# A two-block transformer kernel: the second router by eight-largest and match-replace, and the key stack's load behind the maxima rows

## The reference, cut to what matters

```python
# block 0, attention: 16 heads of depth 8, softmax over 256 keys
scores = einsum('bhtd,bhsd->bhts', q, k) / sqrt(8)
attn = softmax(scores); out = einsum('bhts,bhsd->bhtd', attn, v)
# block 0, feed-forward: 64 experts of hidden size 88, 4 of 8 groups, top 8 experts, plus a shared one
# block 1, attention: a recurrent delta rule over the 16 sequences as time steps
# block 1, feed-forward: 8 experts of hidden size 512 and a ninth gate that scales x itself
probs = softmax(x @ router_w + router_b)               # 9 values per token
top_v, top_i = top_k(probs, 2)                          # the two largest, first index wins a tie
gates = sum(one_hot(top_i, 9) * top_v[..., None], -2)   # 9 gates per token, 7 of them zero
out = einsum(gates[..., :8], y) + gates[..., 8:] * x
```

## Time and profile before

| what | value |
|---|---|
| median of 3 runs | 2077.13 us (2068.6 to 2082.84) |
| the profiled execution's own time | 2077.66 us |
| its span, first to last instruction | 2075.9 us |
| mean granted TensorE clock | 0.926 |
| PE, DVE, ACT, POOL busy | 88%, 70%, 39%, 33% of the span |
| attention | about 50 to 425 us |
| experts, first part | about 545 to 1595 us |

### The profile page before, as it was taken

How to read it: one execution, slowest core, us unless ns; L and a number is a source line. 1 busy time by engine, 2 the same in 40 slices (tenths; PEclk the granted TensorE clock), 3 DMA queues, 4 the chain that set the end, 5 groups by cost and what they waited for, 6 DMA issues and landing times. The chain is left out here.

```text
span 2075.9 us, 25471 instructions
## 1 busy us (share of the span) xinstructions
PE 1825.3 (88%) x7668; PEld 1083.9 (52%) x7668; DVE 1454.5 (70%) x2624; ACT 812.9 (39%) x1501; POOL 682.3 (33%) x610
## 2 busy tenths in 40 slices
PE   2888888851899999989899899998997998999999
PEld 1455455541566656556556465565564554555555
DVE  5776666548666686986968969869689577554444
ACT  1466565631433324324233243332432543443333
POOL 2011111100000491943737718447376076000000
PEclk9988887855799999999999999999998998999999
DMA  7544343010223353323333233333331000000000
GB/s 262 153 115 108 102 116 94 26 70 0 77 106 115 99 175 99 97 78 96 86 87 96 76 96 87 87 96 85 87 97 31 1 5 6 6 6 5 5 5 5
DMA packets 101223, 157.84 MB, mean 76 GB/s; under 512 B 11221, under 2 KB 49454, under 8 KB 97929
## 3 DMA queue, kind: packets, MB, share of 16 engines
q1 hardware_dynamic: 97495, 154.65, 25.3%
q10 hardware_dynamic: 1586, 1.30, 0.2%
q0 software_dynamic: 2048, 0.79, 0.2%
HBM read 123.27 MB, written 33.42 MB: 75 GB/s over the span
## 5 line engine op out<-in xcount | busy, mean ns | idle before, releaser
L1293 PE MATMUL psum<-e_hhi,e_ring 128*128 128x512 f32 x704 | 480.6, 683 | 40.9 <-DVE e_hm L1736 32.0
L1548 ACT ACTIVATE e_gu<-psum 128x512 f32<-128x512 f32 (+1 forms) x368 | 219.0, 597 | 668.1 <-PE psum L1295 527.4
L1302 PE MATMUL psum<-e_hm,w_d 128*128 128x512 f32 (+1 forms) x736 | 383.9, 604 | 14.8 <-DVE e_x L1665 12.2
L1732 DVE TENSOR_TENSOR e_gu<-psum,e_gu 128x512 f32<-128x512 f32 x352 | 241.3, 686 | 185.4 <-PE psum L1332 170.3
L1800 POOL TENSOR_TENSOR e_prod<-e_state,e_phi 128x512 f32<-128x512 f32 x256 | 356.2, 1430 | 5.5 <-DVE e_y L1605 3.2
L1768 DVE TENSOR_TENSOR e_hm<-psum,e_gu 128x512 f32<-128x512 f32 x256 | 175.3, 689 | 206.0 <-ACT e_gu L1573 154.3
L1294 PE MATMUL psum<-e_hhi,e_ring 128*128 128x512 f32 x704 | 282.6, 401 | 0.0
L1295 PE MATMUL psum<-e_hlo,e_ring 128*128 128x512 f32 x704 | 281.7, 400 | 0.0
L1412 PE MATMUL psum<-e_hm,w_gu 128*128 128x512 f32 x512 | 266.8, 607 | 8.6 <-DVE e_hm L1768 3.5
L1573 ACT ACTIVATE e_gu<-psum 128x512 f32<-128x512 f32 x256 | 152.4, 597 | 287.1 <-PE psum L1295 260.8
L1736 DVE TENSOR_TENSOR e_hm<-psum,e_gu 128x512 f32<-128x512 f32 x352 | 243.6, 692 | 12.1
(11 more groups left out here) (238 smaller groups left out, 2482.9 us busy)
## 6 DMA issues: line engine op xcount, KB each, us to landing
e_ring<-w_split SPq DMA_DIRECT2D x308, 256.0 KB, 2.6
qk_parts<-at_part SPq DMA_DIRECT2D x96, 192.0 KB, 2.7
w_split<-e_ring SPq DMA_DIRECT2D x44, 256.0 KB, 2.0
at_qs<-qk_parts SPq DMA_DIRECT2D x16, 576.0 KB
at_ks<-qk_parts SPq DMA_DIRECT2D x16, 576.0 KB
w_gu<-in_w SPq DMA_DIRECT2D x2, 2048.0 KB, 10.6
sel_buf_r<-w_split SPq DMA_DIRECT2D x14, 256.0 KB, 2.6
w_gu<-in_wg SPq DMA_DIRECT2D x1, 2904.0 KB
```

What stands on the lines that cost most here:

```text
L1293: pe.matmul(out, w_hi, x_hi, start=first, stop=False)
L1302: mm = pe.matmul(ps[:, ACC, :], weights_at(T, WD + P * j, P)[0:rows(j), :], hm[0:rows(j), slot(j), :], start=(j == 0), stop=(j == HT - 1))
L1548: a(act_g[0:r, j % 2, :], ps[0:r, GB[j % 2], :], ACT.Silu).then_inc(silu_done, 1)
L1732: ins = v.tensor_tensor(product, ps[0:r, UB[j % 2], :], act_g[0:r, j % 2, :], ALU.mult)
```

## The change

1. In attention, SP's `load_stacks` becomes two loads. The query stack is loaded as before. Then SP waits until half 1 of batch n-1's maxima rows has landed in `at_qs` (`nrows_in[1]`), and only then loads the key stack. The writes of the next batch's parts stand behind that wait in SP's list.
2. The ranking in block 1's router is replaced. At tile 36 four `max` instructions (one for each token tile, nine values in, the eight largest out) stand in place of three comparisons and mask products over 324 values. At tile 37 a `memset` makes the places 2 to 7 of the eight unmatchable and four `match_replace` mark the two largest, in place of an addition and a reduction over 324 values. `router_cut` tests for the mark. The input `less9` and its load are gone; a semaphore `router_turn` is raised twice on the way.

```diff
-            def load_stacks(buf):
-                for stack, q in ((qs, 0), (ks, 1)):
-                    sp.dma_start(stack[0:ROWS, buf, :, :], bounce[buf, q].rearrange("b a d h t -> (b a d) h t")).then_inc(stacked, 16)
+            def load_stack(buf, stack, q):
+                sp.dma_start(stack[0:ROWS, buf, :, :], bounce[buf, q].rearrange("b a d h t -> (b a d) h t")).then_inc(stacked, 16)
...
+                rows_in = held(f"rows_in_{k}", 16 * n)
...
                     sp.wait_ge(part_out, out)
-                    load_stacks((k + 1) % BUFS)
+                    load_stack((k + 1) % BUFS, qs, 0)
+                    if f["p2"]:
+                        sp.wait_ge(nrows_in[1], rows_in)
+                    load_stack((k + 1) % BUFS, ks, 1)
...
-EARLY_LOADS = ("wqkv", "wo", "wr", "b_r1", "less9", "sel1")
+EARLY_LOADS = ("wqkv", "wo", "wr", "b_r1", "sel1")
...
-                s.done(v.tensor_tensor(pairs(above), pa, pb, ALU.is_gt), False)
-                s.done(v.tensor_tensor(pairs(equal), pa, pb, ALU.is_equal))
-                per = lambda ap: ap.rearrange("p (t g) -> p t g", t=CT)
-                s.done(v.tensor_tensor(per(equal), per(equal),
-                                       T["less9"][:].rearrange("p g e -> p (g e)").unsqueeze(1).broadcast_to([P, CT, E1 * E1]), ALU.mult))
+                v.sem_inc(router_turn, 1)
+                for t in range(CT):
+                    s.done(v.max(top[:, t, :], pr[:, t, :]), t == CT - 1)

             def router_rank(s):
-                s.done(v.tensor_tensor(above, above, equal, ALU.add))
-                s.done(v.tensor_reduce(rank[:].rearrange("p t e -> p (t e)"), above.rearrange("p (g e) -> p g e", e=E1), AX.X, ALU.add))
+                s.done(v.memset(top[:, :, TOP1:8], UNMATCHED))
+                v.sem_inc(router_turn, 1)
+                for t in range(CT):
+                    s.done(v.match_replace(out=w1[:, t, :], in_to_replace=top[:, t, :], in_values=pr[:, t, :],
+                                           imm_value=TAKEN), t == CT - 1)

             def router_cut(s):
-                s.done(v.scalar_tensor_tensor(w0[:], rank[:], float(TOP1), pr[:], ALU.is_lt, ALU.mult))
+                s.done(v.scalar_tensor_tensor(w0[:], w1[:], TAKEN / 2, pr[:], ALU.is_lt, ALU.mult))
```

More of the change, by code:

```diff
@@ L1041 @@
 TOP1 = 2
-EARLY_LOADS = ("wqkv", "wo", "wr", "b_r1", "less9", "sel1")
+EARLY_LOADS = ("wqkv", "wo", "wr", "b_r1", "sel1")
 FFN0_LOADS = len(EARLY_LOADS) + 5
-ROUTER_STEPS = 16
+ROUTER_STEPS = 20
 WG, WU, WD = 0, HIDDEN_ALL, 2 * HIDDEN_ALL
@@ L1138, in experts @@
         pr, w0, w1 = (sb(f"e_{n}", [P, CT, E1]) for n in ("pr", "w0", "w1"))
-        rank = w1
-        above = nt[:].rearrange("p t d -> p (t d)")[:, 0:CT * E1 * E1]
-        equal = xc[:, 0:CT * E1 * E1]
+        top = sb("e_top", [P, CT, 8])
         parts = sb("e_parts", [P, CT, PARTS, E1], BF16)
@@ L1179, in experts @@
         r_step = sem("r_step")
+        router_turn = sem("router_turn")
         shifted = sem("shifted")
@@ L1625, in router_gates @@
                 s.done(v.tensor_tensor(pr[:], pr[:], over(rs[:]), ALU.mult))
-                pa = pr[:].unsqueeze(2).broadcast_to([P, CT, E1, E1])
-                pb = pr[:].unsqueeze(3).broadcast_to([P, CT, E1, E1])
-                pairs = lambda ap: ap.rearrange("p (t g e) -> p t g e", g=E1, e=E1)
-                s.done(v.tensor_tensor(pairs(above), pa, pb, ALU.is_gt), False)
-                s.done(v.tensor_tensor(pairs(equal), pa, pb, ALU.is_equal))
-                per = lambda ap: ap.rearrange("p (t g) -> p t g", t=CT)
-                s.done(v.tensor_tensor(per(equal), per(equal),
-                                       T["less9"][:].rearrange("p g e -> p (g e)").unsqueeze(1).broadcast_to([P, CT, E1 * E1]), ALU.mult))
-            def router_rank(s):
-                s.done(v.tensor_tensor(above, above, equal, ALU.add))
-                s.done(v.tensor_reduce(rank[:].rearrange("p t e -> p (t e)"), above.rearrange("p (g e) -> p g e", e=E1), AX.X, ALU.add))
+                v.sem_inc(router_turn, 1)
+                for t in range(CT):
+                    s.done(v.max(top[:, t, :], pr[:, t, :]), t == CT - 1)
+            def router_rank(s):
+                s.done(v.memset(top[:, :, TOP1:8], UNMATCHED))
[3 more added lines that the diff above has]
+                                           imm_value=TAKEN), t == CT - 1)
             def router_cut(s):
-                s.done(v.scalar_tensor_tensor(w0[:], rank[:], float(TOP1), pr[:], ALU.is_lt, ALU.mult))
+                s.done(v.scalar_tensor_tensor(w0[:], w1[:], TAKEN / 2, pr[:], ALU.is_lt, ALU.mult))
                 s.done(v.tensor_copy(parts[:, :, 0, :], w0[:]))
@@ L1844 @@
 NAMES = ("x_fm", "x_tm", "c_fm", "wmod", "w_qk", "b_qk", "w_v", "b_v", "w_fc", "b_fc", "b_o", "ident", "rot", "ident_bf",
-         "gate_w", "gate_b", "wg", "wu", "wd", "sd", "wqkv", "wo", "sel", "wr", "b_r1", "less9", "sel1", "w1", "w2")
+         "gate_w", "gate_b", "wg", "wu", "wd", "sd", "wqkv", "wo", "sel", "wr", "b_r1", "sel1", "w1", "w2")
 def adaln_two_blocks(nc, *args):
@@ L1861, in adaln_two_blocks @@
                                 bfc_col=[P, 1], bo_col=[P, 1], shift=[P, 4, BATCH], scale1=[P, 4, BATCH], gate=[P, 4, BATCH],
-                                eps=[P, 1], ga_bfc=[P, BATCH], ga_bo=[P, BATCH], wqkv=[P, QKV1], wo=[P, D], wr=[P, E1], b_r1=[P, E1],
-                                less9=[P, E1, E1]).items():
+                                eps=[P, 1], ga_bfc=[P, BATCH], ga_bo=[P, BATCH], wqkv=[P, QKV1], wo=[P, D], wr=[P, E1], b_r1=[P, E1]).items():
             sb(name, shape)
@@ L1928, in layout @@
     a["b_r1"] = f(np.broadcast_to(i["L1_ffn_router_b"], (P, E1)))
-    a["less9"] = f(np.broadcast_to(np.tril(np.ones((E1, E1), np.float32), -1), (P, E1, E1)))
     a["sel1"] = f(np.tile(np.broadcast_to(np.eye(E1)[:, :, None], (E1, E1, P)), (PARTS, 1, 1)).astype(bf16))
```

## The result

| | before | after |
|---|---|---|
| median | 2078.98 us, 4 runs (2068.6 to 2082.84) | 2000.52 us, 4 runs (1997.03 to 2004.95) |
| profiled execution's own time, span | 2077.66, 2075.9 | 2004.95, 2003.1 |
| granted clock, whole span | 0.926 | 0.948 |

The kernel is faster by 3.7%: the ratio is 0.9631, with a 95% interval of 0.959 to 0.9672. The forecast was 2013 us in a range of 1986 to 2048.

What follows compares the result with a forecast made beforehand. TensorE, 88% busy, was taken as the bound, standing still for late maxima rows in attention and VectorE's router comparisons in the experts; 34 + 31 = 65 us off 2077.66 gave 2013 us, range 1986 to 2048.

Steps and rivals of the forecast that it cites:

- Attention, 34 us forecast: Attention with the key stack loaded behind the rows: 17 us of waits plus 17 us of clock, 11 to 45.
- The rows are held by the key stack: Attention: half 1's rows' write is 3.1 us late behind the stack loads; afterwards it lands in 1.70 us.
- VectorE's L355 is next, a gain of 1.4 us a batch and not 2.5: Attention: TensorE then waits for VectorE's L355, so 1.4 us a batch is gained, 17 us for twelve batches.
- Half of the clock's 34 us comes back, 17: Attention: the lower clock level costs 34 us in all; half is taken as regained, 17 us, ends 0 and 34.
- rival A: Attention: the rows are not late because of the key stack, so attention gives nothing: 2047 us, chance 0.09.
- The router, 31 us forecast: Block 1's router with the new ranking: 26 us from six chunks plus 5 us from chunk 6, 22 to 51.
- MAX8 and match-replace cost what block 0's rows say, GpSimd or not: Router: four MAX8 take 0.37 us, match-replace 0.85 us, not held by GpSimd; 6 x 4.25 = 26 us gained.
- No gain by the clock: Router: VectorE sets the pace where the clock is 0.50, so nothing is taken for clock; upper end 16 us.
- Chunk 6, 5 us: Router in chunk 6: the wait is 2.89 us; a gain of 5 us with the clock, 2 to 9.
- B: Router: MAX8 and match-replace are held by GpSimd, so only attention pays: 2044 us, chance 0.09.
- D: Whole change: neither part pays, VectorE's and ScalarE's lists being just as late behind each repaired wait: 2075 us, chance 0.06.
- C: Attention: the wait moves from half 1's rows to half 0's and the kernel is slower: 2093 us, chance 0.04.

Runs made afterwards that it cites:

- experiment 1: The kernel before with only the attention part of the change, the key stack loaded after half 1's rows: 2037.0 us, ratio 0.981 to the kernel before.
- experiment 3: The changed kernel with the key stack's heads 0 to 7 loaded right behind the query stack, heads 8 to 15 behind the rows: 1995.24 us.
- Experiment 2: The kernel before with only the router part of the change: 2042.66 us, ratio 0.9844 to the kernel before.
- experiment 4: The changed kernel with both stacks loaded only after half 1's rows have landed: 2020.33 us, ratio 0.9723 to the kernel before.
- experiment 8: The changed kernel with attention's third rest behind the maxima of heads 8 to 11 and router_cut at tile 38 instead of 40: 1980.21 us.

## Why the prediction held, step by step

**Attention, 34 us forecast.** 36.6 in the profile, 36.3 between the means of three profiles with the old code and three with the new, 40 in experiment 1. *The rows are held by the key stack*: shown by experiments 1 and 3; landing after 1.73 us of idle time where 1.70 was forecast. *VectorE's L355 is next, a gain of 1.4 us a batch and not 2.5*: L263 waits 1.19 us, and TensorE's idle time fell by 1.3 a batch. Two of the 15 waits of the earlier trace rows were at head 0 and not at head 8 as the prediction read them, 2.6 of its 34.8 us. *Half of the clock's 34 us comes back, 17*: 1.6 us a batch is 19 for twelve. Both terms were right within 2 us; the second by luck, since no row carried the choice of "half". What was off is small: half 0's L460 comes 0.9 to 1.2 us later after its write and not 0.2, since the key load runs beside SP's writes. It cost next to nothing: TensorE's waits for the rows at head 0 sum to 1.3 us in the changed kernel and to 3.6 in experiment 1, against 2.6 before. That the rows "speak against" turns between queues, as the prediction says under rival A, doesn't follow: experiment 3 shows in which order the write was served, and not that such turns are absent.

**The router, 31 us forecast.** 34.2 in the profile. *MAX8 and match-replace cost what block 0's rows say, GpSimd or not*: 0.38 against 0.37 us, and the rank 0.89 (842.41 to the next product at 843.30) against 0.85. The rule of the Trainium skill that the prediction named ("SBUF — State Buffer", Who interferes with whom) agrees, with 152 ns beside GpSimd. Counted from L1628 (L1625 before), tile 37's product comes 3.95 us earlier, tile 38's 4.07 and tile 41's still 4.08, so VectorE does set the pace here, as the forecast had it: 4.1 of 5.6 us. *TensorE would wait about 0.7 us*: 0.89. *No gain by the clock*: here the step failed in its reason and, by 1.5 us a chunk, in its size. TensorE's wait for the second product fell by 4.2 us, but 2.3 of it moved to L1393 (0.78 before, 3.16 after in chunk 0), where time at the lower clock, 6.8 us a chunk at the router before and 4.3 after, made up only a part. The end of the chunk, which the forecast left as it was, gave the rest: 1.2 us of wait on average (1.6 in the chunk shown), and in the middle chunks its 3.4 us at the lower clock. In six chunks that makes 27.5 us for the 26 forecast, uneven: 3.2, four times about 5.6, and 2.0. Experiment 2, with the same router, had 5.2 for the last of these, so its 2.0 is a matter of one chunk end in one execution. *Chunk 6, 5 us*: 5.9. Its wait of 2.89 us is gone, one for L1594 a little later grew from 0.79 to 1.68, and the time at the lower clock beside them fell from 13.7 to 3.4 us.

**The rivals.** A, B and D are shut out by experiments 1 and 2. C didn't come about, and experiment 4 shows it as a real mechanism one load further on.

The forecast's sum was 12.5 us too slow in the median. Some 3 us are attention, 3 the router, 2 `route0`; the rest is between the profiled executions and the medians (2004.95 against 2000.52).

## What to carry to other kernels

Before an engine's instruction is made smaller, look at what runs beside it: the same three comparisons fell from 1.5 to 0.49 us by standing two tiles later, and that was most of what the new instructions gave. A small transfer that is on the critical path should be issued ahead of a large one even if it has a queue of its own, and the large one only waits until the small one has landed, not longer: one stack behind the rows was right, two were not. When a wait goes, count the next two that the same engine will meet, since idle time reappears there, and read the granted clock behind each.

## What was not expected of the hardware

- A CAST of 36 values with one SBUF input was held by GpSimd as a two-input instruction is: 967 ns against 185 when GpSimd is idle, beside 152 ns for MAX8. One SBUF input is thus not enough to be free of it. The Trainium skill ("SBUF — State Buffer", Who interferes with whom) names casts among the operations that can enter a two-port mode and then contend with GpSimd, which would fit; no run here tells the mode.
- The clock's level in attention differs between profiles of the same code: new code 4.27, 2.56 and 3.41 us a batch at the lower level (lengths 20.14, 19.61 and 19.85 us). One profile of a stage is no measure of 5 us.
- With 6 TensorE waits over 1 us left from 86 to 360 us in experiment 8 (7.3 us, against 14 with 31.5 us before), the clock there rose to 0.98, from 0.84: the idle time taken away came back once more as clock.
